# Reordering the first layer of a four-layer attention kernel: side work between attention steps, next tokens normed early

## What is computed

```python
xn = layer_norm(x, gamma_pt)
q, k, v, ff = split(xn @ w_fused, [1024, 1088, 1152])   # 16 heads of 64, one key/value head
q, k = apply_rope(pos, q) * scale, apply_rope(pos, k)
attn = softmax(where(causal, -neg, q @ k.T))
y = x + (attn @ v) @ w_attn_out + silu(ff_gate) * ff_val @ w_ff_out
yn, ctx = layer_norm(y, gamma_ca), layer_norm(context, gamma_ctx)
cq = (yn @ w_q) * scale
ck, cv = split(ctx @ w_kv, 2)                            # one key/value head of 64
cout = softmax(cq @ ck.T) @ cv @ w_out
fv, fg = split(yn @ w_ff1, 2)
out = y + cout + silu(fg) * fv @ w_ff2
```

## Time and profile before

| | us |
|---|---|
| median of 3 runs | 4416.52 (4416.21 to 4422.58) |
| the profiled execution | 4412.29 |
| its span | 4410.4 |
| TensorE busy | 3961.4 (90%) |
| its weight loads busy | 3237.9 (73%) |
| VectorE busy | 1888.1 (43%) |
| ScalarE busy | 1624.9 (37%) |
| GpSimd busy | 317.7 (7%) |
| mean granted TensorE clock | 0.945 |

### The profile page before, as it was taken

The page is one execution under the profiler, slowest core; times in us unless marked ns, Lnnn a source line. Parts: engine busy times, 40 slices in busy tenths (PEclk is TensorE's granted clock), DMA queues, the critical chain, the costliest instruction groups (busy, mean ns, idle before and its releaser), DMA issues. The chain is left out here.

```text
span 4410.4 us, 69236 instructions
## 1 busy us (share of the span) xinstructions
PE 3961.4 (90%) x23128; PEld 3237.9 (73%) x23128; DVE 1888.1 (43%) x5419; ACT 1624.9 (37%) x3709; POOL 317.7 (7%) x379
## 2 busy tenths in 40 slices
PE   7988988989888899999997799999999998888888
PEld 6877787878777688888875577777777676666666
DVE  3444445434534455555554233233232332555644
ACT  2232222322322333433332344544444443333333
POOL 1000000000000111111100000000000000111110
PEclk9998999989999899999998999999999999899989
DMA  4000000000000200000001100000000000000000
GB/s 160 3 10 7 9 10 3 10 12 3 10 3 22 92 12 11 11 7 11 11 2 37 44 7 6 12 7 6 12 7 6 12 7 13 19 11 15 18 13 5
DMA packets 63988, 74.90 MB, mean 17 GB/s; under 512 B 8336, under 2 KB 61168, under 8 KB 62704
## 3 DMA queue, kind: packets, MB, share of 16 engines
q1 hardware_dynamic: 63728, 71.42, 5.2%
HBM read 64.01 MB, written 7.40 MB: 16 GB/s over the span
## 5 line engine op out<-in xcount | busy, mean ns | idle before, releaser
L309 PEld LDWEIGHTS l_bank<-identity,l_p 112*125 112x125 f32 (+1 forms) x3456 | 523.2, 180 | 315.2 <-ACT l_p L362 63.3
L161 PE MATMUL l_bank<-l_xT,weights_of_layers_and 128*128 128x224 f32 x3072 | 650.0, 371 | 43.0 <-ACT l_xT L748 19.5
L331 PE MATMUL l_bank<-l_cv,l_pT 125*112 125x65 f32 (+2 forms) x5376 | 640.1, 253 | 50.3 <-ACT l_pT L372 45.1
L161 PEld LDWEIGHTS l_bank<-l_xT,weights_of_layers_and 128*128 128x128 f32 x3072 | 600.8, 199 | 69.2 <-ACT l_xT L748 24.0
L331 PEld LDWEIGHTS l_bank<-l_cv,l_pT 125*112 125x112 f32 x5376 | 601.9, 178 | 63.1 <-ACT l_pT L372 31.5
L309 PE MATMUL l_bank<-identity,l_p 112*125 112x112 f32 (+1 forms) x3456 | 555.0, 273 | 75.1 <-ACT l_p L362 69.7
L369 ACT ACTIVATE l_p<-l_bank,l_nm 112x375 f32<-112x375 f32 x512 | 291.9, 573 | 477.7 <-DVE l_nm L396 477.2
L299 PE MATMUL l_bank<-l_ckT,l_qz 128*112 128x375 f32 x1024 | 424.3, 498 | 7.2 <-DVE l_qz L1297 7.2
L366 ACT ACTIVATE l_p<-l_p,l_nm 112x375 f32<-112x375 f32 x384 | 233.1, 607 | 474.5 <-DVE l_nm L393 473.3
L396 DVE TENSOR_REDUCE l_nm<-l_bank 112x1 f32<-112x375 f32 x512 | 279.0, 548 | 207.2 <-PE l_bank L299 202.8
L362 ACT ACTIVATE l_p<-l_p,l_nm 112x112 f32<-112x112 f32 x768 | 234.3, 376 | 304.6 <-DVE l_nm L389 303.4
(11 more groups left out here) (242 smaller groups left out, 4709.1 us busy)
## 6 DMA issues: line engine op xcount, KB each, us to landing
l_cx<-in_ctx SPq DMA_DIRECT2D x64, 375.0 KB
x_after_layer<-l_z SPq DMA_DIRECT2D x24, 224.0 KB, 2.4
l_x<-x_after_layer SPq DMA_DIRECT2D x24, 224.0 KB, 2.7
weights_of_layers_and<-in_L_xattn_w_fused SPq DMA_DIRECT2D x1, 2048.0 KB, 16.4
weights_of_layers_and<-in_L_xattn_w_ff SPq DMA_DIRECT2D x1, 2048.0 KB, 11.9
weights_of_layers_and<-in_L_xattn_lin_W SPq DMA_DIRECT2D x2, 1024.0 KB, 9.9
weights_of_layers_and<-in_L_xattn_sa_wkv SPq DMA_DIRECT2D x1, 2048.0 KB, 16.2
weights_of_layers_and<-in_L_xattn_ca_wkv SPq DMA_DIRECT2D x1, 2048.0 KB, 20.7
```

Of the source, the lines that this page charges most:

```text
L161: last = pe.matmul(out, left, right, start=(k == 0), stop=(k == len(pairs) - 1))
L309: last = pe.transpose(bank[:ph.keys, g * T:(g + 1) * T], p[:, m % PD, g * ph.keys:(g + 1) * ph.keys], ident[:T, :T])
L331: last = pe.matmul(bank[:T, g * w:(g + 1) * w], pT[:ph.keys, m % PD, t * T:(t + 1) * T], ph.val(j, r, t), start=(t == 0), stop=(t == ph.ti ...
```

## The change

In `layer0` the same operations are issued in another order, and the rings are cut anew:

- The banks are now 2 for scores, 2 for turned probabilities, 4 for products.
- In step s of self attention (s = 0 to 7) TensorE projects `f{s}` after its attention work; its tanh and gate follow in the next step (`amid`, ahead of ScalarE's exponentials and behind VectorE's maxima). Steps 1 to 4 also turn one context tile each, step 8 the outputs of the first sequence.
- `outputs` issues the `hid` products of y and z first and waits for the turned outputs only after them; y0 runs ahead of the turning of the second sequence's outputs, z0 too.
- The context key and value products stand around `yT`; `cf6` and `cf7` move into steps 0 and 1 of cross attention, the first sequence's `cOT` into steps 22 and 26.
- The next turn's x is measured in step 8 and centred in step 12 of cross attention; `xT` is turned in step 30. The next turn's k is projected ahead of z0, its v and q0 between z0 and z1, its q1 to q3 behind z1. The next context is measured by VectorE after z0 and centred after q1.
- So a loop turn now begins with self attention. A prologue (turn -1) norms and projects the first tokens, and the last turn is written out behind the loop of 7.
- SP loads the first context ahead of the first weights.
- `Attention.tensor`, `scalar` and `vector` take a list of phases and the hook `amid`; layers 1 to 3 pass one phase and keep their order.

The core of the diff:

```diff
-    def lagged(self, ph, steps, between=None):
-        for k in range(ph.items + LAG_V):
+    def lagged(self, phases, steps, between=None, amid=None):
+        items = [(ph, k) for ph in phases for k in range(ph.items)]
+        for n in range(len(items) + LAG_V):
             for lag, step in steps:
-                if 0 <= k - lag < ph.items:
-                    step(k - lag)
+                if step is amid:
+                    if amid:
+                        amid(n)
+                elif 0 <= n - lag < len(items):
+                    step(*items[n - lag])
...
+        beside_own = {s: [(f"f{s}", "dve")] for s in range(8)}
+        for n, name in enumerate(("cT00", "cT01", "cT10", "cT11")):
+            beside_own[n + 1].append((name, "act"))
+        beside_own[8] = [("OT00", "act"), ("OT01", "act")]
+        chain = [("y0", "dve"), ("OT10", "act"), ("OT11", "act"), ("y1", "dve"), ("ck0", "act"), ("cv0", "act"), ("ck1", "act"), ("yT", "act"), ("cv1", "act")] \
+            + [(f"cq{t}", "act") for t in range(4)] + [(f"cf{f}", "dve") for f in range(6)]
+        beside_cross = {0: [("cf6", "dve")], 1: [("cf7", "dve")], 22: [("cOT00", "act")], 26: [("cOT01", "act")], 30: [("xT", "act")]}
+        ending = [("k", "dve"), ("z0", "dve"), ("cOT10", "act"), ("cOT11", "act"), ("v0", "act"), ("v1", "act"), ("q0a", "dve"), ("q0b", "dve"), ("z1", "dve")] \
+            + [(f"q{t}{s}", "dve") for t in (1, 2, 3) for s in "ab"]
...
-        P = Ring(ctx, nc, "l0_product", banks[5:8],
-        A = Attention(ctx, nc, "l0", [own, cross], banks[0:3], banks[3:5], P)
+        P = Ring(ctx, nc, "l0_product", banks[4:8], jobs)
+        A = Attention(ctx, nc, "l0", [own, cross], banks[0:2], banks[2:4], P)
...
             sp.dma_start(x[:, :, :], xv[0]).then_inc(x_come.sem, 16)
+            load_context(0)
             weights.issue(sp, "first")
-            load_context(0)
...
+            def outputs(i, name, j, wo, wff, hidden, turned):
+                for sem, count in P.free(i, name, P.got(hidden)):
+                    pe.wait_ge(sem, count)
+                bank = P.bank(name)[:T, 0:D]
+                for f in range(8):
+                    pe.matmul(bank, hid[:, f, j * T:(j + 1) * T], wff[:, f, :], start=(f == 0), stop=False)
+                pe.wait_ge(P.emptier(turned).sem, P.count_emptied(i, turned))
+                for t in range(8):
+                    last = pe.matmul(bank, OT[:, j, t, :], wo[:, t, :], start=False, stop=(t == 7))
+                last.then_inc(P.full.sem, 1)
...
+            def own_side(i, s):
+                if s < 8:
+                    project(pe, P, i, f"f{s}", [columns(V["wff"], s), columns(V["wff"], 8 + s)], xT)
+                if 1 <= s <= 4:
+                    context_turned(i, (s - 1) // KT, (s - 1) % KT)
+                if s == 8:
+                    for half in range(2):
+                        output_turned(i, 0, half, f"OT0{half}", own.job(own.groups - 1))
+
+            def cross_side(i, s, coming):
+                if s < 2:
+                    gate_and_value(i, 6 + s)
+                elif s in (22, 26):
+                    output_turned(i, 0, (s - 22) // 4, f"cOT0{(s - 22) // 4}", cross.job(H - 1))
+                elif s == 30:
+                    if coming:
+                        turn_tokens(pe, c, P, i, "xT", xhat, normed.this(NORMS.index("x")))
+                    else:
+                        P.pass_over(pe, "pe", i, ["xT"])
+
+            def turn_ending(i, coming):
+                if coming:
+                    keys(i)
...
+                outputs(i, "z0", 0, V["wo2"], V["wf2"], "cf7", "cOT01")
+                for half in range(2):
+                    output_turned(i, 1, half, f"cOT1{half}", cross.job(cross.items - 1))
+                if coming:
+                    values(i)
+                    queries(i, 0)
...
+                outputs(i, "z1", 1, V["wo2"], V["wf2"], "cf7", "cOT11")
+                if coming:
+                    for t in (1, 2, 3):
+                        queries(i, t)
...
+            def cross_side(i, s, coming):
+                if s < 2:
+                    hidden(i, 14 + s)
+                elif coming and s == 8:
+                    measure_x(i)
+                elif coming and s == 12:
+                    center(i, "x", batches(x), batches(xhat))
+
+            def turn_ending(i, coming):
+                if coming:
+                    keys_turned(i)
...
+                add(i, "z0", 0, z, y)
+                if coming:
+                    measure_context(i)
+                    queries_turned(i, 0)
...
+                add(i, "z1", 1, z, y)
+                if coming:
+                    queries_turned(i, 1)
+                    center(i, "c", context_rows, context_rows)
+                    queries_turned(i, 2)
+                    queries_turned(i, 3)
```

More of the change, by code:

```diff
@@ L336, in values @@
                 last.then_inc(self.values.sem, 1)
-        self.lagged(ph, [(0, scores), (LAG_T, turns), (LAG_V, values)], between)
+        self.lagged(phases, [(0, scores), (LAG_T, turns), (LAG_V, values)], between)
     def turned(self, eng, i, ph, k, copy):
@@ new lines, in layer0 @@
+        jobs = [job for s in range(own.items + LAG_V) for job in own_job(s) + beside_own.get(s, [])] + chain \
+            + [job for s in range(cross.items + LAG_V) for job in cross_job(s) + beside_cross.get(s, [])] + ending
+        names = [job for job, _ in jobs]
+        before_x = names[:names.index("xT")]
+        after_x = names[names.index("xT") + 1:names.index("k")]
+        P = Ring(ctx, nc, "l0_product", banks[4:8], jobs)
+        A = Attention(ctx, nc, "l0", [own, cross], banks[0:2], banks[2:4], P)
@@ L676, in outputs @@
[L676 to L689 removed]
+                roots(i, "y")
@@ L691, in _ @@
+                coming(i)
+                pool_steps.end()
+            pool_steps.start(TURNS - 1)
+            roots(TURNS - 1, "y")
         @block.tensor
         def _(pe):
[L693 to L697 removed]
+            def outputs(i, name, j, wo, wff, hidden, turned):
[8 more added lines that the diff above has]
+                last.then_inc(P.full.sem, 1)
@@ new lines, in turn @@
+            def turn(i, coming):
+                A.tensor(pe, i, [own], c.ident, lambda s: own_side(i, s))
+                between_phases(i)
+                A.tensor(pe, i, [cross], c.ident, lambda s: cross_side(i, s, coming))
+                turn_ending(i, coming)
+            prime(pe, "pe", [A.S, A.TR], [A.values])
+            pe.wait_ge(zeroed, 4)
+            P.pass_over(pe, "pe", -1, before_x)
+            turn_tokens(pe, c, P, -1, "xT", xhat, normed.this(NORMS.index("x")))
+            P.pass_over(pe, "pe", -1, after_x)
@@ new lines, in _ @@
+            pe.wait_ge(weights.sems["first"], weights.count("first"))
+            keys(-1)
+            P.pass_over(pe, "pe", -1, ["z0", "cOT10", "cOT11"])
+            values(-1)
+            pe.wait_ge(swapped, 1)
+            queries(-1, 0)
+            P.pass_over(pe, "pe", -1, ["z1"])
+            for t in (1, 2, 3):
+                queries(-1, t)
+            pe.wait_ge(weights.sems["ff"], weights.count("ff"))
+            with pe.Fori(0, TURNS - 1) as i:
+                turn(i, True)
@@ L753, in gates, with _, tokens_turned, gate @@
+            turn(TURNS - 1, False)
+        @block.scalar
+        def _(act):
+            def tokens_turned(i, name, g):
+                act.wait_ge(P.full.sem, P.count_full(i, name))
+                for t in range(KT):
+                    last = act.activation(xT[:, t, :], P.bank(name)[:, t * TP:(t + 1) * TP], ACT.Copy, scale=g[:, t:t + 1])
+                last.then_inc(P.emptier(name).sem, 1)
+            def gate(i, n):
+                pre, f = ("c" if n >= 8 else ""), n % 8
                 name = f"{pre}f{f}"
@@ new lines, in values, with gate_before, own_side @@
+            def values(i):
+                for j in range(PAIR):
+                    act.wait_ge(P.full.sem, P.count_full(i, f"v{j}"))
+                    act.activation(v[:, j, 0:DH], P.bank(f"v{j}")[:T, 0:DH], ACT.Copy).then_inc(P.emptier(f"v{j}").sem, 1)
+            def gate_before(i, s):
+                if 1 <= s <= 8:
+                    gate(i, s - 1)
+            def own_side(i, s):
+                if 1 <= s <= 4:
+                    context_turned(i, (s - 1) // KT, (s - 1) % KT)
+                if s == 8:
+                    for half in range(2):
+                        output_turned(i, 0, half, f"OT0{half}")
@@ L868, in _ @@
-                dve.wait_ge(rooted.sem, rooted.count(i, 2))
-                for j in range(PAIR):
-                    last = center(xhat[:, j, :], y[:, j, :], j, 2, T)
-                last.then_inc(normed.sem, 1)
-                hidden(i, "c", 8)
-                A.vector(dve, i, cross, dve_steps)
-                dve.wait_ge(z_sent.sem, z_sent.count_before(i))
-                for j in range(PAIR):
-                    dve.wait_ge(P.full.sem, P.count_full(i, f"z{j}"))
```

(11 more changed lines are left out.)

497 lines of the change are left out of this document (275 added, 222 removed).

## The result

| | before | after |
|---|---|---|
| median | 4419.55 us (4416.21 to 4425.81) | 4243.99 us (4238.64 to 4250.89), ratio 0.9602, interval 0.9581 to 0.9623 |
| profiled execution, span | 4412.29, 4410.4 | 4239.7, 4238.0 |
| last product of the first layer ends | 1415.75 | 1252.41 |
| the rest of the span | 2994.6 | 2985.6 |
| a turn of the first layer | 173.7 to 178.1 | 150.2 (first), 151.8 to 154.2 |

What follows compares the result with a forecast made beforehand. TensorE's own stream bounds the first layer, so its interruptions can be won: waits 139.6 plus clock 43.6, less residual 11.2 and prologue 2.2, gain 169.8 us; 4412.3 becomes 4242.5, median 4246, range 4228 to 4288 (own case 4230 to 4258).

Steps and rivals of the forecast that it cites:

- Work of a turn, 150.5: First layer: TensorE's work in one turn at full clock sums to 150.5 us, 1204 over eight turns.
- Clock: First layer: 46 us of TensorE's busy time came from half clock after idling; all but 2.4 would go, gaining 43.6.
- The first rival: Clock still falls behind self attention's tail, slowing the y product 3 us a turn: +24, 4270 us; chance 0.16.
- Residual waits: TensorE waits left per turn: 0.4 yT, 0.4 self attention tail, 0.4 edge, 0.2 small ones; 11.2 us in all.
- the second rival: Waits of another kind remain, TensorE behind ScalarE's one queue, as in the third layer: +22, 4268 us; chance 0.19.
- Loop edge: VectorE's 2.6 to 2.9 us issue at 7 edges now precedes the first maxima; cost 0.2 to 2.9, taken 0.4.
- The rival on the edge: TensorE itself stops at 7 loop edges for 2.6 to 2.9 us each: +19, 4265 us; chance 0.06.
- the crossing at 2951.13: Third layer: TensorE crosses its loop edge to the first scores without idle time, taken as evidence against TensorE stopping.
- Prologue: Context loaded ahead of the first layer's first weights delays the start: bounds 0 and 5.0 us, taken 2.2.
- the issue row: Loading the context first costs 1.61 us of issue; the 2.2 us taken for the start was set nearest this.
- Banks, VectorE's load, statistics of x, order of y and z: First layer: fewer score banks, early token norm in cross attention and reordered outputs cost 0 to 0.1 us, taken as nothing.
- The slack of the product ring: Four product banks: the nearest case, last context turning against f3's gate, keeps about 0.4 us slack, so cost 0.

Runs made afterwards that it cites:

- The fillers: Kernel before the change, with 12 unused products ahead of each token turning and 16 ahead of the first turning of probabilities: 4396.42 us, ratio 0.9940.
- 64 memsets: Changed kernel with 64 one-element fills on VectorE ahead of its first-layer loop, moving the code behind them: 4223.55 us, ratio 0.9554.

## Why the prediction held, and where its steps were off

The forecast was 4246 (the sum gives 4246.7), the median is 4244. The gain was put at 169.8 us and is 172.4; in the layer itself it is 163.3, so 6.5 less, and 9.0 that were in no sum came from outside. The steps:

- **Work of a turn, 150.5.** Confirmed within 1 us. The first turn, without an edge, takes 150.2, of which 0.66 are the two small waits below: 149.5 of work. Written out on VectorE, the first six turns take 150.07 to 150.26. The term gives 7.6 us more than taken over eight turns (0.95 each).
- **Clock.** The gain in busy time, 156.3 to 149.8 a turn, is 6.5; 5.75 was taken (46 over eight turns), the rest is in the line above. All turns stay at 0.99 or 1.00. The first rival falls: behind the tail of self attention, at 228 to 240 us, the clock is 1.00, and the y product that now follows it takes 3.66 us for the 16 instructions of its `hid` part, about the 3.62 of full clock. Its mechanism is real, though: with the f projections back in one piece, and the small waits with them, the clock falls behind the tail. The fillers show the term by itself, at 4.3 a turn where waits remain.
- **Residual waits.** 0.4 behind yT: it is 0.21. 0.4 at the tail of self attention: nothing, the second rival falls too. Not foreseen: 0.45 us at the start of each cross attention, where the first products with values wait for VectorE's copy (L335, 3.6 in 8; before had 4.3 in 8 one step earlier, and cf6 and cf7 were to cover it). Together 0.66 where 1.0 was taken: 2.7 us to the good.
- **Loop edge: the step that failed in size.** Taken 0.4 a turn in seven edges, 2.8 us; it is 2.7 (152.9 - 150.2) in six, 16.0. The count was wrong, since the last turn now stands behind the loop. The price was within its bounds of 0.2 to 2.9, but for a cause that these bounds did not know: they priced a stall of the 2.6 to 2.9 us that the earlier trace rows shows, and the stall itself became 4.8 to 5.0, since the new code lies elsewhere. At 2.8 us it costs 0.5, near what was taken. The rival on the edge had the order of its price right (+19, where 13.2 came) and its mechanism wrong at five edges of six: TensorE crosses in 0.22 to 0.73 us there, and VectorE is what stops. At the fifth TensorE does stop, for 1.86 us, and with banks 3, 2 and 3 it does at all six (1.7 to 2.2); the crossing at 2951.13 was no proof that it never will. That a taken branch to a target outside the fetched window stalls its engine for a fetch is what the Trainium skill says ("Runtime: NRT & Kernel Launch", section "Instruction fetch mechanics"); the trace agrees, by the unrolled kernel and by the packets of q14 at the edges. That section of the Trainium skill has the fetch in blocks of 256 instructions; for VectorE the shifts show a period of 128 and the packets have 8192 bytes, and there the measurement decides.
- **Prologue.** Taken 2.2, bounds 0 and 5.0; it is 5.1 (30.41 against 25.29), by experiment 5.3. The choice of the issue row as the nearer one was wrong, and so was the upper bound by a little: the weights land 5.0 us later than in before (the swap starts at 27.41 against 22.38), about the sum of both rows (1.61 + 3.4). Behind the context SP's next issue, of the cosines, takes 2.95 us where it took 0.45, so not all of the loss is at the context's own issue.
- **Banks, VectorE's load, statistics of x, order of y and z.** Taken at nothing; all hold but for the score banks at the loop edge, where the third group of scores waits for one of the two (3.4 us in 5, counted in the edge). VectorE has no wait of its own making in the cross attention, and heads stay 1.54 us apart. The slack of the product ring, put at 0.4, was real: one bank less turns it into 24.8 us of waits.
- **The other layers, -9.0.** No term. In the third layer the wait of 21.9 us behind the context copies and one of 6.6 before the first turned probabilities became these (waits view, TensorE, 2230 to 3570):

```profile
PE l_bank L161 <- ACT l_cT L2047: 17.8, 16, 1.6
...
PE l_bank L313 <- ACT l_p L366: 3.2, 8, 0.4
```

That is 7.5 of the 9.0, in unchanged code. Across the kernels run here that rest takes 2970.7 to 3007.5 us; nearly all of this spread is in TensorE's busy time (2687.8 to 2722.6), which goes with its granted clock there (0.951 to 0.938). VectorE's edge stalls are not a likely cause: with 64 memsets six stalls of 2.7 to 3.0 us in the second layer and 60 packets of q14 behind the first layer are gone, and the rest is no shorter (2990.0 against 2985.6). What shortened the two waits stays open.

The errors: 13.2 (edge) and 2.9 (prologue) against, 7.6 and 2.7 for, 5.8 in sum, where the layer misses 6.5; the other layers' 9.0 hid it. So the hit at 4244 is better than its parts, and part of it is luck.

Put together as parts, the early norm of the tokens (45.6), the f projections between the steps (48.5) and the fourth bank (32.6, which only serves those projections) account for about 94 of 163 us; they were each taken out alone, such numbers do not add exactly, and the second is net of the edge that it lays bare. The rest is, as what is left over, the context's norm moved away from the first maxima, which the kernel with the f projections in one piece shows only by its missing wait: no run has that move alone undone.

## What to carry over

A gap on TensorE costs its length and, where the clock falls, a few us more behind it: fill gaps with work that is ready, even before the critical path needs it. A loop edge stalls an engine that jumps back to the loop's start, and the length of the stall changes with the place of the code: put the edge where that engine is ahead, and time a version with its turns written out, or shifted by half a period. Price a bank that is moved between rings by who releases it, not by how many there are.

## What the runs showed of the hardware

- VectorE's stall at a loop edge has two levels, 2.4 to 2.9 and 4.7 to 5.0 us, and repeats when its code is shifted by 128 instructions. At the long level two packets of q14 are waited for, one behind the other, their starts 2.4 to 2.7 us apart; at the short one, one. The page's count of instruction transfers of after fits that, with 1.01 MB in 123 packets, 8.2 KB each, and of the other queue 2.67 MB in 163, 16.4 KB:

```profile
q8 instruction: 163, 2.67, 0.3%
q14 instruction: 123, 1.01, 0.1%
```

  If an instruction takes 64 bytes, which is what the Trainium skill's section named above comes to (16 KiB for 256), then 8.2 KB are by estimate 128 instructions. By their times the packets of q14 are VectorE's; whose the others are no view shows. With VectorE's turns written out the second line has 103 packets: 20 fewer, all in the first layer, though its code there is longer. With 64 memsets it has 63.
- With the tokens normed late the clock is at 0.50 when work resumes behind the gap of 3.29 us (184 to 190 us; key projection 3.36 us for 8). At the fifth edge of after it is at 0.50 behind one gap of 1.86 us; the 0.97, 0.89 and 0.37 of the other edges, with work between, leave the windows at 1.00.
- Adding 10.8 us of unused products to each turn shortened it by 4.3 us.
